# A tokenizer's third depthwise stage moved from VectorE and GpSimd to TensorE with diagonal matrices

## The reference, cut to what matters

```python
def dwconv(x, wd, wp, bp):
    y = conv(x, wd, pad=((1, 1), (1, 1)), groups=x.shape[1])
    return conv(y, wp, bp)
...
h = (1.0 - gate) * loc + gate * glob
h = jax.nn.relu(dwconv(h, f1_dw, f1_pw, f1_pwb))
h = jax.nn.relu(dwconv(h, f2_dw, f2_pw, f2_pwb))
h = dwconv(loc + h, f3_dw, f3_pw, f3_pwb)
```

## Time and profile before

| | us |
|---|---|
| median of 3 runs | 1386.32 |
| lowest, highest | 1379.9, 1394.95 |
| profiled execution, its own time | 1390.42 |
| its span in the profile | 1388.6 |

### The profile page before, as it was taken

One profiled execution on the slowest core, in us unless ns is written; L12 is line 12 of the kernel. 1 busy time (PEld: TensorE's weight loads), 2 busy tenths in 40 slices (PEclk: granted clock), 3 DMA queues, 4 the chain that ended last, 5 costly groups with the idle time before them and its releaser, 6 DMA issues.

```text
span 1388.6 us, 19388 instructions
## 1 busy us (share of the span) xinstructions
PE 1204.5 (87%) x5756; PEld 778.7 (56%) x5757; DVE 1022.9 (74%) x1934; ACT 705.8 (51%) x1490; POOL 778.9 (56%) x501
## 2 busy tenths in 40 slices
PE   7986636478898989898987799999999899999996
PEld 4432324234454545455443468888888677777774
DVE  5999797998898999999999736678788653333332
ACT  1356551776767777676856245545453332222221
POOL 3148992878878696959698310135455574222222
PEclk9985656798999999999999999999998799999998
DMA  6200001440404132231410001122222132222221
GB/s 182 59 0 0 30 10 45 170 146 1 147 1 146 34 113 77 69 99 47 141 37 0 0 28 43 42 65 59 56 67 74 43 57 47 37 36 38 36 35 21
DMA packets 72800, 81.17 MB, mean 58 GB/s; under 512 B 13282, under 2 KB 64705, under 8 KB 72721
## 3 DMA queue, kind: packets, MB, share of 16 engines
q1 hardware_dynamic: 53386, 69.29, 16.0%
q0 software_dynamic: 17152, 9.24, 4.9%
q10 hardware_dynamic: 2184, 1.72, 0.5%
HBM read 48.87 MB, written 30.01 MB: 57 GB/s over the span
## 4 chain that ended last, share of the span: by engine, by line
PE 58%; DVE 21%; ACT 9%; issue 6%; POOL 4%; DMA 1%; DVEq 0%; SPq 0%; POOLq 0%; ACTq 0%
PE ps L2196 10%; PE ps L980 7%; PE ps L2215 6%; DVE hs L1263 6%; PE ps L1580 3%; PE ps L1638 3%; DVE ps L184 3%; PE ps L891 3%; PE ps L1653 3%; PE ps L247 3%; PE ps L2205 2%; ACT ps L1133 2%; PE ps L957 2%; PE ps L916 2%; PE ps L934 2%
## 5 line engine op out<-in xcount | busy, mean ns | idle before, releaser
L1381 POOL TENSOR_TENSOR Bx<-dtz,Bb 128x984 f32<-128x984 f32 x128 | 289.5, 2281 | 43.4 <-DVE hs L1263 29.9
L1263 DVE TENSOR_TENSOR_SCAN hs<-ps,Bx 128x492 f32<-128x492 f32 x256 | 287.7, 1165 | 22.1 <-POOL Bx L1381 12.8
L1133 ACT ACTIVATE ps<-dt,A 128x324 f32<-128x324 f32 (+1 forms) x512 | 211.4, 456 | 77.9 <-DVE hs L1263 76.9
L980 PE MATMUL ps<-hs,b_id 128*128 128x492 f32 x512 | 240.4, 592 | 11.7 <-DVE y L1230 9.0
L2315 POOL DMA_INDIRECT out<-yt,dest x48 | 74.7, 1556 | 172.8 <-DVE yt L2301 160.5
L1273 DVE TENSOR_TENSOR hs<-hs,ps 128x984 f32<-128x984 f32 x128 | 150.3, 1174 | 2.8 <-issue 0.8
L2196 PE MATMUL ps<-W,xT 97*128 (+1 forms) x384 | 143.2, 516 | 3.6 <-issue 2.4
L980 PEld LDWEIGHTS ps<-hs,b_id 128*128 128x128 f32 x512 | 93.3, 195 | 79.6 <-issue 74.3
L2285 DVE COPY hT__5811<-ps 128x768 f32<-128x768 f32 x48 | 46.0, 958 | 114.2 <-PE ps L2205 112.8
L2253 ACT ACTIVATE hb<-ps 128x768 f32<-128x768 f32 x48 | 38.9, 810 | 142.9 <-PE ps L2196 142.9
L2215 PE MATMUL ps<-W,hT__5811 128*128 x576 | 109.3, 327 | 0.8 <-DVE yb L2295 0.8
(11 more groups left out here) (273 smaller groups left out, 2387.1 us busy)
## 6 DMA issues: line engine op xcount, KB each, us to landing
Bb<-b_rows SPq DMA_DIRECT2D x32, 656.0 KB, 6.8
buckets<-b_zero SPq DMA_DIRECT2D x8, 2288.0 KB, 15.4
xg<-buckets SPq DMA_DIRECT2D x48, 104.0 KB
xc<-in_xcol SPq DMA_DIRECT2D x4, 1176.0 KB, 9.2
W<-in_w1d SPq DMA_DIRECT2D x8, 582.0 KB
W<-in_w2d SPq DMA_DIRECT2D x8, 576.0 KB
out<-H SPq DMA_DIRECT2D x8, 246.0 KB
H<-P SPq DMA_DIRECT2D x8, 147.0 KB
```

Of the source, the lines that this page charges most:

```text
L980: mm = pe.matmul(ps[:, BANK_Y + h, 0:HALF], ident[:], f2(hs[:, s % LONG])[:, h * HALF:(h + 1) * HALF], start=s == 0, stop=s == STATE - 1)
L1133: a = act.activation(ps[:, BANK_A + h, c:c + w].rearrange("p (g t) -> p g t", t=S)[:, :, 1:S], dt[:, (par + t // STATE) % 2, m, g0 * S:g1 ...
L1263: v.tensor_tensor_scan(f2(hs[:, t % LONG])[:, c], ps[:, BANK_A + h, 0:HALF], f2(Bx[:, t % RING])[:, c], 0.0, ALU.mult, ALU.add).then_inc(s ...
L1381: g.tensor_tensor(Bx[:, t % RING], dtz[:, p], Bb[:, p, t % STATE, :].rearrange("p (a n) -> p a n", a=1).broadcast_to([128, NI, N]), ALU.mu ...
```

## The change

For the third fusion stage both tiles are now computed by TensorE. A depthwise tap is a product with a diagonal matrix, so nine matmuls of a 96x96 diagonal on the nine shifted views add up in one PSUM bank (taps, 441 columns). ScalarE makes the 18 diagonals once, from the identity with the weight column as its scale (diagonals, behind its work of wave 2), and copies each sum from PSUM to where the third layer reads it (keep_taps). third_sums, the third add_up and the third weigh are gone. The bank for the taps is one of the three that the third layer's fills used, so two are left for them. The order in each list is in the diff; the rest follows the new semaphores (s_tapped counts groups of nine, s_kept the copies). The diagonals lie in memory that the patches' input used before.

```diff
+        diag = sb("diag", [HD, 2, 9, HD])
...
-        f3_bank = [psC[0:TWO, 0, 0:2 * D], psC[0:TWO, 1, 0:2 * D], psC[0:TWO, 2, 0:2 * D]]
+        f3_bank = [psC[0:TWO, 0, 0:2 * D], psC[0:TWO, 1, 0:2 * D]]
+        tap_bank = psC[0:HD, 2, 0:ROWS * GRID].rearrange("p (r c) -> p r c", c=GRID)
...
-        s_dwf = [sem(f"a_dwf{k}") for k in range(3)]
+        s_dwf = [sem(f"a_dwf{k}") for k in range(2)]
+        s_diag = sem("a_diag"); s_tapped = sem("a_tapped"); s_kept = sem("a_kept")
...
-            return sum(0 <= w_ - k_ - 1 < CH for w_ in range(w + 1) for k_ in range(3) if (w_, k_) < (w, k))
+            return sum(0 <= w_ - k_ - 1 < CH for w_ in range(w + 1) for k_ in range(2) if (w_, k_) < (w, k))
...
+            def taps(c, k):
+
+                pe.wait_ge(s_diag, 1)
+                pe.wait_ge(s_lr, c + 1)
+                pe.wait_ge(s_gelu, 3 * CH)
+                if c + k > 0:
+                    pe.wait_ge(s_kept, 2 * c + k)
+                for t in range(9):
+                    mm = pe.matmul(tap_bank, diag[:, k, t, :], tap(PF[2], k, c, t), start=t == 0, stop=t == 8)
+                mm.then_inc(s_tapped, 1)
...
                     pair(psA, wf[:, 0], lambda k: G2[:, k, :]).then_inc(s_w2, 1)
+                if 0 <= w - 3 < CH:
+                    taps(w - 3, 0)
                 if 0 <= w - 1 < CH:
...
                     pair(psB, wf[:, 1], lambda k: dense(DF[0], k)).then_inc(s_f[0], 1)
+                if 0 <= w - 3 < CH:
+                    taps(w - 3, 1)
                 if 0 <= w - 2 < CH:
...
                 if 0 <= w - 3 < CH:
                     c = w - 3
-                    pe.wait_ge(s_dwf[2], c + 1)
-                    pe.wait_ge(s_sum, 8 * (tiles_before(w, 2) + 1))
-                    if c == 0:
-                        pe.wait_ge(s_gelu, 3 * CH)
+                    pe.wait_ge(s_kept, 2 * c + 2)
                     for n in range(c * FILLS, (c + 1) * FILLS):
-                        if n >= 3:
-                            pe.wait_ge(s_t0, n - 2)
+                        if n >= 2:
+                            pe.wait_ge(s_t0, n - 1)
                         for j in range(2):
                             b = 4 * n + 2 * j - c * IM
                             for k in range(2):
                                 both = last_sums(c)[:, k].rearrange("p r c -> p (r c)")[:, b * ROW * GRID:b * ROW * GRID + TWO]
-                                mm = pe.matmul(f3_bank[n % 3][:, j * D:(j + 1) * D], both,
+                                mm = pe.matmul(f3_bank[n % 2][:, j * D:(j + 1) * D], both,
                                                wf[:, 3, k, :], start=k == 0, stop=k == 1)
                         mm.then_inc(s_f[2], 1)
...
+            def keep_taps(c, k):
+
+                act.wait_ge(s_tapped, 2 * c + k + 1)
+                if c > 0 and k == 0:
+                    act.wait_ge(*last_read(c))
+                act.activation(last_sums(c)[:, k, 0:ROWS, :], tap_bank, ACT.Copy).then_inc(s_kept, 1)
+
+            def diagonals():
+
+                act.wait_ge(s_conv, 3 * CH)
+                for k in range(2):
+                    for t in range(9):
+                        col = V_F_DW + 36 + 9 * k + t
+                        i = act.activation(diag[:, k, t, :], ident[0:HD, 0:HD], ACT.Copy, scale=vec[0:HD, col:col + 1])
+                i.then_inc(s_diag, 1)
...
                 if 0 <= w - 1 < CH:
                     act.wait_ge(s_h, w)
                     weigh(0, w)
+                if CH <= w < WAVES - 1:
+                    keep_taps(w - 3, 0)
                 if 0 <= w - 2 < CH:
                     act.wait_ge(s_r1, w - 1)
                     weigh(1, w)
-                if 0 <= w - 3 < CH:
-                    act.wait_ge(s_lr, w - 2)
-                    weigh(2, w)
                 if w == WAVES - 1:
+                    keep_taps(CH - 1, 0)
+                    keep_taps(CH - 1, 1)
                     tail("last wave")
...
                     i.then_inc(s_tg, 1)
+                if w == CH - 1:
+                    keep_taps(0, 0)
                 if 0 <= w - 1 < CH:
...
                     i.then_inc(s_r1, 1)
+                if 0 <= w - 3 < CH - 1:
+                    keep_taps(w - 3, 1)
                 if 0 <= w - 2 < CH:
...
                     i.then_inc(s_r2, 1)
+                if w == CH - 2:
+                    diagonals()
...
-            def third_sums(c):
-
-                v.wait_ge(s_lr, c + 1)
-                dw(v, own, PF[2], last_sums(c), (0,), c, V_F_DW + 36, s_dwf[2], read=(lambda k: last_read(c)) if c > 0 else None)
...
             for w in range(CH + 1):
                 if w < CH:
                     local_sums(w)
@@ -479,15 +512,11 @@
                     take_rows(0)
                 if w >= 2:
                     second_sums(w - 2)
-                if w >= 3:
-                    third_sums(w - 3)
             second_sums(CH - 1)
             norm_rows(0)
             take_rows(1)
             tail("last but one taps")
-            third_sums(CH - 2)
             norm_rows(1)
-            third_sums(CH - 1)
...
-                out = (last_sums(w - 3) if k == 2 else DF[k])[:, 1, 0:ROWS, :]
+                out = DF[k][:, 1, 0:ROWS, :]
...
-                for k in range(3):
+                for k in range(2):
                     if 0 <= w - k - 1 < CH:
                         if w - k - 1 > 0:
-                            g.wait_ge(*(last_read(w - 3) if k == 2 else (s_f[k], w - k - 1)))
+                            g.wait_ge(s_f[k], w - k - 1)
                         add_up(k, w)
...
-                    v.wait_ge(tok.s_sum, 8 * 3 * CH)
+                    v.wait_ge(tok.s_sum, 8 * 2 * CH)
...
-                g.wait_ge(tok.s_dwf[2], CH)
+                g.wait_ge(tok.s_tapped, 2 * CH)
...
+    first["diag"] = -(-first["sg"] // 64) * 64
```

More of the change, by code:

```diff
@@ L431, in take_rows @@
                     v.wait_ge(s_f[2], n + 1)
-                    v.tensor_tensor(T0[:, 2 * n:2 * n + 2, :], f3_bank[n % 3].rearrange("p (j c) -> p j c", j=2),
+                    v.tensor_tensor(T0[:, 2 * n:2 * n + 2, :], f3_bank[n % 2].rearrange("p (j c) -> p j c", j=2),
                                     rows[:, 0:1, :].broadcast_to([TWO, 2, D]), ALU.add).then_inc(s_t0, 1)
@@ L553, in tokenizer @@
         tok.sync, tok.tensor, tok.scalar, tok.vector, tok.gpsimd, tok.sems = sync, tensor, scalar, vector, gpsimd, sems
-        tok.s_out, tok.s_cls, tok.s_t0, tok.s_lr, tok.s_sum, tok.s_dwf, tok.s_t1 = s_out, s_cls, s_t0, s_lr, s_sum, s_dwf, s_t1
+        tok.s_out, tok.s_cls, tok.s_t0, tok.s_lr, tok.s_sum, tok.s_tapped, tok.s_t1 = s_out, s_cls, s_t0, s_lr, s_sum, s_tapped, s_t1
         return tok
@@ L2452, in places @@
     first["oh"] = first["rl"]
+    first["diag"] = -(-first["sg"] // 64) * 64
+    assert early["xc"] <= first["diag"] and first["diag"] + 18 * HD * F <= first["wzg"] and first["wzg"] <= early["D1"]
     assert top <= late["L2"] and first["Bb"] < early["PF0"]
```

## The result

| | before | changed |
|---|---|---|
| median of 4 runs each, us | 1390.63 | 1404.51 |
| lowest, highest | 1379.90, 1396.31 | 1398.74, 1406.63 |
| profiled execution, its own time | 1390.42 | 1403.23 |
| its span | 1388.6 | 1401.3 |

The ratio is 1.0102, with a 95% interval from 1.0059 to 1.0145: the change costs 14 us (8 to 20). The forecast was 1384 us, some 3 us under the 1386.3 that three runs of the kernel before had given (a fourth makes their median 1390.6), and its range ended at 1400.

The account below looks back on a forecast made before the run. VectorE looked like the wall, GpSimd close behind. Of VectorE's 19.8 us removed only 2.8 would arrive, as a serial chain of taps, copies, products and additions took over: 1386.3 to 1383.5, rounded to 1384 us, range 1371 to 1400.

Parts of the forecast that it names:

- (a): TensorE's eight groups of nine diagonal products: about 3.4 us a group at the full clock, 6.8 at the half.
- Rival 2: Tap groups run at the half clock, five on the walk, 3.4 us more each: 17 us, so 1400 us; chance 0.22.
- step 2: TensorE in wave 3: a tap group ahead of each fusion pair, making the reader L414 6.3 us late.
- step 4: Wave 4: taps(1,1) to 176.3 ahead of the second fusion pair, which ends at 179.0; L543 1.9 us late.
- step 5: taps(2,0) waits for L543, products wait for its copy; GpSimd starts at 187.3 instead of 181.68; L543 1.9 us late again.
- step 6: Chunk 3's two tap groups, their copies and four L1065 precede the transposes, which start 1.6 us late.
- (b): ScalarE makes 18 diagonals of 96 columns: 5.0 us, with ends of 3.6 and 8.3.
- (c): ScalarE's eight copies of 441 columns out of PSUM: 0.6 us each.
- (e): The third layer has two banks for its fills instead of three: costed at nothing.
- Rival 3: Diagonals at 8.3 us and slower ScalarE copies: 3 to 5 us more, no change, 1388 us; 0.68 together with the forecast.
- (d): New waits: each TensorE tap group waits for ScalarE's previous copy; copies precede GpSimd's products; no separate size given.
- Rival 1: VectorE stays the wall and only its work counts: 22 us less, 1364 us; chance 0.10.

Follow-up runs that it names:

- x3_banks_diag: The kernel before with the 18 diagonals made but not used and two fill banks for the third layer instead of three; ratio to before 1.0014.
- x4_late: The changed kernel with five of the eight tap groups later in TensorE's list, behind or between the fusion pairs; ratio to before 1.0060.
- x11_short_tile1: The kernel before with ScalarE's products and GpSimd's additions 2 to 8 of the third stage (tile 1) on one row of 63; ratio to before 0.9956.
- x12_short_tile0: The kernel before with VectorE's taps 1 to 7 of the third stage (tile 0) on one row of 63; ratio to before 0.9928.
- x5_tile1_pe: x4_late with only tile 1 (GpSimd's and ScalarE's part) on TensorE, nine diagonals, VectorE keeping third_sums; ratio to before 0.9921.
- x6_tile0_pe: x4_late with only tile 0 (VectorE's part) on TensorE, nine diagonals, tile 1 staying with ScalarE and GpSimd; ratio to before 1.0016.

## Why the prediction was wrong

**(a), the price of a tap group: this term failed.** It read the rows rightly, 0.34 us for one matmul instruction of a pair at the full clock, and then multiplied by the 9 products that the code writes. The rows count instructions. A float32 product is two of them, so a group is 18 instructions: 18 x 0.33 x 441/392 = 6.7 us, and the profile has 6.67 to 6.89. The sentence of the kernel's description that calls a pair eight matmuls has the same slip: it is four calls. The forecast had 3.4, and took 0.5 us for one matmul as the sign of the half rate. The instructions show 0.37, which looks like a hit if the count isn't read with it.

**Rival 2's sum came true by another cause.** It had 6.8 us a group, five groups on the walk, 17 us more and 1400. The clock had no part in it: PEclk was 0.93 over the stage, and every group but the first ran at the full rate. The five groups named, (0,0), (0,1), (2,0), (3,0), (3,1), were those on the walk, and (1,1) joined them: GpSimd's addition for the second pair of wave 4 ended at 184.9 and the pair started at 187.35, behind the group, 2.5 us later. In all 5 x 3.5 + 2.5 = 20.0 of the 22.1 us by which the walk exceeds the forecast's. Seen from the forecast's 2.8 us of gain that is 17 us of loss; 14 (8 to 20) were measured.

**The walk, step by step.** Times from the start of L414 or L450 of wave 2:

| event (step) | forecast | changed | late |
|---|---|---|---|
| products of wave 3 end (1) | 16.2 | 15.8 | -0.4 |
| GpSimd's L536, now L565 (1) | 26.2 | 25.8 | -0.4 |
| VectorE's next taps (1) | 28.2 | 27.9 | -0.3 |
| second pair of wave 3 ends (2) | 37.3 | 43.8 | 6.5 |
| GpSimd's two additions end (3) | 58.0 | 64.5 | 6.5 |
| second pair of wave 4 ends (4) | 60.9 | 69.7 | 8.8 |
| GpSimd's last eight additions start (5) | 69.2 | 81.6 | 12.4 |
| L543, now L572, ends (5) | 86.1 | 100.0 | 13.9 |
| hn of the first images done (6) | 96.0 | 116.9 | 20.9 |
| second projection (7) | 102.8 | 124.8 | 22.1 |

Each jump is a group or two: 6.8 at step 2 (two groups, from -0.3 to 6.5), 2.3 at step 4, 3.6 at step 5, 7.0 at step 6 (two groups). Between the jumps the lag stands still, but for 1.5 us while GpSimd adds beside VectorE and TensorE does its last pair, and 1.2 between hn and z.

**(b), (c), (e).** 18 diagonals took 4.88 us (forecast 5.0), a copy 0.54 (0.6), and the lost bank nothing that shows:

```profile
121.39 4.88 ACT L392 ACTIVATE diag<-b_id,vec 96x96 f32<-96x96 f32 x18
...
152.34 0.54 ACT L384 ACTIVATE DF<-ps 96x441 f32<-96x441 f32 x1 [6.15 <-PE ps L269]
```

Rival 3's premise, diagonals at 8.3 us and slower copies, did not come. What the diagonals of 4.88 us and the two banks cost the whole is not resolved: the ratio of x3_banks_diag leaves room for -4 to 8 us.

**(d), the waits in the order of the engines.** Putting five of the groups later gave back 10.6 us of the walk (7.7 by VectorE's start) in one profile of x4_late; the ratios, with overlapping intervals, don't show it.

**The bound.** Rival 1 (VectorE the wall, 22 us to gain) was refused for the right reason: VectorE is busy 38 of 73.5 us now, not nine tenths. For the kernel before, x11_short_tile1 and x12_short_tile0 show VectorE as the wall, GpSimd close behind it, and GpSimd's load making VectorE's row work dearer. The prediction saw the last (4.48 against 1.41 us) and counted it for nothing, which was right for the changed kernel, where VectorE idled 17.55 us ahead of z; in x5_tile1_pe it is a good part of the gain.

## What to carry to other kernels

Before a new use of an engine is priced from a row, count in the code how many calls made that row's instructions: a float32 matmul call is two of them, so a row's mean times the calls is half the price. Where two engines share a stage and both are near full, move the share of the one whose work also slows the other, and only as much as the third engine can do beside them: half of this change, in the order of x4_late, was worth 1%, and the whole cost 1%. New work for an engine belongs behind the results for which others wait; the profiles of x4_late and x6_tile0_pe point that way, the ratios don't settle it.

## What was not expected of the hardware

- **Two instructions for a float32 product.** At the full clock each took 0.37 us on 441 columns (6.67 us for 18), so 0.74 a product; a bf16 product was one of 0.23 (2.08 us for 9, with the end of the last, where a float32 group so measured is 6.87). The Trainium skill (FP8 and Floating Point Precision, TensorE Precision Notes) says that true FP32 takes four passes through the array. By that rule, the trace agrees: four passes of 441 columns at 2.4 GHz are an estimated 0.735 us, against 0.74. The prediction had not weighed it.
- **Short runs in the moving operand cost nothing here.** It is read 7 of 8 elements at a time; 0.371 us an instruction is the 0.330 of the pairs (2.64 for 8), read in runs of 49, times 441/392.
- **Rows beside GpSimd.** Four L480, the former L442, took 3.93 us with GpSimd adding and 1.41 with it idle (4.48 and 1.41 before), which is how x5_tile1_pe took most of its 7.8 us off VectorE:

```profile
169.07 3.93 DVE L480 SCALAR_TENSOR_TENSOR P<-P,mv,rows 105x192 f32<-105x192 f32 x4
...
198.76 1.41 DVE L480 SCALAR_TENSOR_TENSOR P<-P,mv,rows 105x192 f32<-105x192 f32 x4
```

- **The same code, up to 10 us apart.** The start of L414 of wave 2 (118.1 to 128.1 us) differs from profile to profile, with no instruction changed ahead of it; why was not followed. A single profile set against another by its absolute times would have made or hidden an effect of this size.
